# Experts' second layer of a mixture-of-experts stage: full-precision products replaced by split fp32r products, with the results of GELU split in two

## What is computed

```python
h   = gelu(einsum('ecd,edf->ecf', xb, fc_w) + fc_b)      # 192 -> 768
out = einsum('ecf,efd->ecd', h, pj_w) + pj_b             # 768 -> 192, the second layer
y   = einsum('nec,ecd->nd', cb_weight, out)              # weighted back to the tokens
```

## Time and profile before

| what | value |
|---|---|
| runs (3): median, lowest, highest | 1009.45, 1009.11, 1009.66 us |
| the profiled execution's own time | 1016.04 us |
| its span, first to last instruction | 1014.3 us |
| mean granted TensorE clock, share of full speed | 0.923 |

### The profile page before, as it was taken

How to read it: one execution, slowest core, us unless ns; L and a number is a source line. 1 busy time by engine, 2 the same in 40 slices (tenths; PEclk the granted TensorE clock), 3 DMA queues, 4 the chain that set the end, 5 groups by cost and what they waited for, 6 DMA issues and landing times.

```text
span 1014.3 us, 21583 instructions
## 1 busy us (share of the span) xinstructions
PE 897.5 (88%) x7037; PEld 698.7 (69%) x7038; DVE 653.3 (64%) x3059; ACT 647.0 (64%) x1379; POOL 504.4 (50%) x549
## 2 busy tenths in 40 slices
PE   3387979999999979999999999367999999999996
PEld 2255556566666656677776776256999999999896
DVE  1676888998998877778877776673344343343341
ACT  2047778886989888988888889165345345344441
POOL 7677746765221201144234333415677677667654
PEclk8577998998999979999999999758999999999999
DMA  7234332322110200010011102427455456554443
GB/s 201 60 75 79 48 63 42 60 62 29 33 32 8 58 1 2 2 38 17 23 39 38 38 3 73 74 56 110 59 109 109 65 110 90 87 109 92 55 50 32
DMA packets 63300, 59.12 MB, mean 58 GB/s; under 512 B 17471, under 2 KB 54242, under 8 KB 63202
## 3 DMA queue, kind: packets, MB, share of 16 engines
q0 software_dynamic: 26624, 29.20, 20.0%
q1 hardware_dynamic: 36386, 28.44, 10.9%
q10 hardware_dynamic: 192, 0.26, 0.1%
HBM read 35.18 MB, written 16.39 MB: 51 GB/s over the span
## 4 chain that ended last, share of the span: by engine, by line
PE 62%; DVE 13%; ACT 5%; issue 3%; POOL 1%; DMA 0%; another core or an unknown queue 0%; POOLq 0%; DVEq 0%; ACTq 0%
PE ps_scores L798 14%; PE ps_ring L790 11%; PE ps_ring L1068 10%; PE ps_ring L798 6%; PE ps_ctx L927 5%; PE ps_scores L910 5%; PE ps_scores L1068 4%; PE ps_scores L913 4%; DVE probs L1456 2%; DVE probs L1470 1%; ACT probs L1170 1%; DVE k L1377 1%; PE ps_ring L873 1%; PE ps_ctx L790 1%; DVE probs L1450 1%
## 5 line engine op out<-in xcount | busy, mean ns | idle before, releaser
L1292 ACT ACTIVATE probs<-ps_scores,fc_bias 128x512 f32<-128x512 f32 (+1 forms) x144 | 88.7, 617 | 172.2 <-PE ps_scores L798 153.9
L661 POOL DMA_INDIRECT out<-z_t,slots_now x80 | 127.8, 1597 | 83.7 <-DVE z_t L1809 59.6
L1152 ACT ACTIVATE prob_t<-ps_ring 128x512 f32<-128x512 f32 x192 | 114.5, 597 | 36.0 <-PE ps_ring L790 35.4
L790 PE MATMUL ps_ring<-ident,probs 128*128 128x128 f32 x768 | 127.6, 292 | 9.0 <-DVE x_hi L1348 4.5
L1177 ACT ACTIVATE probs<-probs,neg_max 128x128 f32<-128x128 f32 x384 | 120.9, 398 | 2.6 <-DVE neg_max L1456 2.5
L1161 ACT ACTIVATE square<-ps_scores 128x512 f32<-128x512 f32 x192 | 104.9, 601 | 25.4 <-PE ps_scores L910 20.0
L1068 PE MATMUL ps_ring<-work,probs 128*128 128x192 f32 x672 | 114.5, 326 | 0.0
L790 PEld LDWEIGHTS ps_ring<-ident,probs 128*128 128x128 f32 x768 | 90.8, 147 | 34.1 <-issue 15.5
L1456 DVE CUSTOM_DVE_ANT_0 probs<-ps_scores,causal 128x128 f32<-128x128 f32 x384 | 88.5, 286 | 39.6 <-PE ps_scores L913 39.1
L1068 PEld LDWEIGHTS ps_ring<-work,probs 128*128 128x128 f32 x672 | 109.3, 190 | 0.1
L798 PE MATMUL ps_scores<-x_hi,fc_hi 128*128 128x512 f32 (+1 forms) x288 | 105.1, 371 | 3.8 <-DVE x_hi L1793 2.6
(11 more groups left out here) (232 smaller groups left out, 2074.0 us busy)
## 6 DMA issues: line engine op xcount, KB each, us to landing
work<-pj_w SPq DMA_DIRECT2D x8, 576.0 KB
k<-k_signed SPq DMA_DIRECT2D x136, 32.0 KB
token_in<-xin SPq DMA_DIRECT2D x8, 384.0 KB, 3.3
out<-resid SPq DMA_DIRECT2D x8, 384.0 KB, 4.2
vals<-fc_w SPq DMA_DIRECT2D x8, 384.0 KB
vals<-fc_w SPq DMA_DIRECT2D x16, 192.0 KB
k<-k_signed POOLq DMA_DIRECT2D x40, 32.0 KB, 2.0
out<-z_t,slots_now POOLq DMA_INDIRECT x80, 3.6
```

Of the source, the lines that this page charges most:

```text
L661: gp.indirect_dma_start(out[:, :], bass.IndirectOffsetOnAxis(slots_now[:, u, 1, t:t + 1], 0), slot_y[:, o, :], None, compute_op=ALU.add).t ...
L790: return pe.transpose(dst, src, ident[0:n, 0:n])
L1152: sc.activation(prob_t[:, s % 2, :, :], src.rearrange("p (h q) -> p h q", h=4), ACT.Exp if p is mag else ACT.Copy).then_inc(ring_free[i], 1)
L1292: sc.activation(hidden[:, c % 2, f_, 0:128 * nt], ps_scores[:, i, 0:128 * nt], ACT.Gelu, bias=fc_bias[:, e, f_:f_ + 1]).then_inc(gelu_done ...
```

## The change

The second layer is written as a split product too. The second weights are rounded by ACT to fp32r (`second_weights_high`) and DVE writes the rest beside them (`second_weights_low`), so that `pj_split` holds for each of six blocks 192 rounded columns and 192 columns of rest. Each of GELU's results is rounded by ACT (`hidden_high`, an ACT copy of the block to `hid_hi`), one block behind the GELUs, and DVE subtracts (`hidden_low`, to `hid_lo`). For each tile PE then multiplies the six rounded blocks by all 384 columns and the six rests by the first 192 columns: 12 matmuls, in the order five rounded, six rests, the last rounded. The rest's rest is left out. `add_bias` adds both halves of the 384 columns of the result, with one more DVE instruction. SP waits for `pj_low` in place of `pj_used`. The tiles' places in memory are rearranged so that `hid_hi`, `hid_lo` and `pj_split` lie where the attention's q, k and the tiles `xin`, `w_hi`, `square` were.

```diff
@@ SyncE
-                sp.wait_ge(pj_used[e % 2], e // 2 + 1)
+                if e > 1:
+                    sp.wait_ge(pj_low, e - 1)
                 load_second_layer(e)
@@ TensorE
             def second_layer(r, u, e, c):
                 t0, nt = CHUNKS[c]
                 if c == 0:
-                    pe.wait_ge(pj_loaded[u], 16 * r + 16)
+                    pe.wait_ge(pj_low, e + 1)
+                order = ([(hid_hi, hid_high, f_) for f_ in range(FF_CHUNKS - 1)]
+                         + [(hid_lo, hid_low, f_) for f_ in range(FF_CHUNKS)] + [(hid_hi, hid_high, FF_CHUNKS - 1)])
...
-                    for f_ in range(FF_CHUNKS):
+                    for k, (part, made, f_) in enumerate(order):
                         if t == t0:
-                            pe.wait_ge(gelu_done[f_ % FC_RING], e * 6 + 2 * c + f_ // FC_RING + 2)
-                        last = pe.matmul(ps_y[i][:, 0:HID], hidden[:, c % 2, f_, tok], pj_w_sb[:, u, f_, :],
-                                         start=(f_ == 0), stop=(f_ == FF_CHUNKS - 1))
+                            pe.wait_ge(made, e * 18 + 6 * c + f_ + 1)
+                        n = 2 * HID if part is hid_hi else HID
+                        last = pe.matmul(ps_y[i][:, 0:n], part[:, f_, tok], pj_split[:, u, f_, 0:n],
+                                         start=(k == 0), stop=(k == 2 * FF_CHUNKS - 1))
@@ ScalarE, in gelus
                     sc.activation(hidden[:, c % 2, f_, 0:128 * nt], ps_scores[:, i, 0:128 * nt], ACT.Gelu,
                                   bias=fc_bias[:, e, f_:f_ + 1]).then_inc(gelu_done[i], 1)
+                    if f_ > 0:
+                        hidden_high(e, c, f_ - 1)
+                hidden_high(e, c, FF_CHUNKS - 1)
+
+            def hidden_high(e, c, f_):
+                tok = slice(0, 128 * CHUNKS[c][1])
+                act.wait_ge(gelu_done[f_ % FC_RING], e * 6 + 2 * c + f_ // FC_RING + 2)
+                apart(act)
+                sc.activation(hid_hi[:, f_, tok], hidden[:, c % 2, f_, tok], ACT.Copy).then_inc(hid_high, 1)
+
+            def second_weights_high(n, u):
+                act.wait_ge(pj_loaded[u], 16 * n + 16)
+                sc.activation(pj_split[:, u, :, 0:HID], pj_w_sb[:, u, :, :], ACT.Copy).then_inc(pj_high, 1)
@@ ScalarE, in expert
                     expert_weights_high(e + 1, 1 - u)
+                    second_weights_high(r + u, 1 - u)
@@ VectorE, in add_bias
-                        ve.tensor_tensor(slot_y[:, o, :], ps_y[i][:, 0:HID], pj_bias[:, e, :], ALU.add
+                        ve.tensor_tensor(slot_y[:, o, :], ps_y[i][:, HID:2 * HID], pj_bias[:, e, :], ALU.add
+                                         ).then_inc(y_begun, 1)
+                        dve.wait_ge(y_begun, CAP_TILES * e + t + 1)
+                        ve.tensor_tensor(slot_y[:, o, :], slot_y[:, o, :], ps_y[i][:, 0:HID], ALU.add
                                          ).then_inc(y_free[i], 1)
@@ VectorE
+                def hidden_low(e, c):
+                    tok = slice(0, 128 * CHUNKS[c][1])
+                    for f_ in range(FF_CHUNKS):
+                        dve.wait_ge(hid_high, e * 18 + 6 * c + f_ + 1)
+                        apart(dve)
+                        ve.tensor_tensor(hid_lo[:, f_, tok], hidden[:, c % 2, f_, tok], f(hid_hi[:, f_, tok]),
+                                         ALU.subtract).then_inc(hid_low, 1)
+
+                def second_weights_low(e, u):
+                    dve.wait_ge(pj_high, e + 1)
+                    apart(dve)
+                    ve.tensor_tensor(pj_split[:, u, :, HID:2 * HID], pj_w_sb[:, u, :, :],
+                                     f(pj_split[:, u, :, 0:HID]), ALU.subtract).then_inc(pj_low, 1)
+
                 def expert(e, u, more):
+                    hidden_low(e, 0)
                     split_x(e, u, 1)
                     add_bias(e, u, 0)
                     if more:
                         split_weights(e + 1, 1 - u)
+                        second_weights_low(e + 1, 1 - u)
+                    hidden_low(e, 1)
                     split_x(e, u, 2)
                     add_bias(e, u, 1)
+                    hidden_low(e, 2)
                     if more:
                         split_x(e + 1, 1 - u, 0)
                     add_bias(e, u, 2)
```

More of the change, by code:

```diff
@@ L192, in tower_kernel @@
         resid = sb("resid", [128, SEQS, HID])
-        xin = sb("xin", [128, SEQS, WITH_GATE])
+        with ExitStack() as attention_only:
+            early = lambda name, shape, dt=F32: attention_only.enter_context(nc.sbuf_tensor(name, shape, dt))
+            q_of = [early(f"q{u}", [128, BLOCKS, GROUP, 128]) for u in range(2)]
+            k_of = [early(f"k{u}", [128, BLOCKS, 2, GROUP, 128]) for u in range(2)]
+            xin = early("xin", [128, SEQS, WITH_GATE])
+            w_hi = early("w_hi", [128, 2, 2, 384], F32R)
+            square = early("square", [128, 2, 4, 2, 128])
+        low_hot_at = sb("low_hot", [128, BLOCKS * GROUP * 128], F32R)
+        high_hot_at = sb("high_hot", [128, BLOCKS * GROUP * 128], F32R)
+        fc_hi = sb("fc_hi", [128, 2, 2, FF], F32R)
+        fc_lo = sb("fc_lo", [128, 2, 2, FF], F32R)
+        hid_hi = sb("hid_hi", [128, FF_CHUNKS, 512], F32R)
+        hid_lo = sb("hid_lo", [128, FF_CHUNKS, 512], F32R)
+        pj_split = sb("pj_split", [128, 2, FF_CHUNKS, 2 * HID], F32R)
         logits = sb("logits", [128, 2, EXPERTS])
@@ L239, in tower_kernel @@
                      for u in range(2)]
-        with ExitStack() as attention_only:
-            early = lambda name, shape: attention_only.enter_context(nc.sbuf_tensor(name, shape, F32))
-            q_of = [early(f"q{u}", [128, BLOCKS, GROUP, 128]) for u in range(2)]
-            k_of = [early(f"k{u}", [128, BLOCKS, 2, GROUP, 128]) for u in range(2)]
-        low_hot_at = sb("low_hot", [128, BLOCKS * GROUP * 128], F32R)
-        high_hot_at = sb("high_hot", [128, BLOCKS * GROUP * 128], F32R)
-        fc_hi = sb("fc_hi", [128, 2, 2, FF], F32R)
-        fc_lo = sb("fc_lo", [128, 2, 2, FF], F32R)
         vals_of = [vals[:, :, :, :], work[:, 2560:4096].rearrange("p (s h d) -> p s h d", s=GROUP, h=HEADS)]
@@ L412, in tower_kernel @@
         pj_loaded = [sem(f"pj_loaded{u}") for u in range(2)]
-        pj_used = [sem(f"pj_used{u}") for u in range(2)]
+        pj_high = sem("pj_high")
+        pj_low = sem("pj_low")
+        hid_high = sem("hid_high")
+        hid_low = sem("hid_low")
+        y_begun = sem("y_begun")
         x_loaded = [sem(f"x_loaded{c}") for c in range(3)]
@@ L790, in transpose, with split_product @@
                 return pe.transpose(dst, src, ident[0:n, 0:n])
-            def split_product(dst, x, w_cols, v, begun=None):
+            def split_product(dst, x, w_cols, v):
                 pairs = ((x[0], w_cols[0]), (x[0], w_cols[1]), (x[1], w_cols[0]), (x[2], w_cols[2]),
@@ L798, in split_product @@
                     last = pe.matmul(dst, lhs, rhs, start=(k == 0), stop=(k == 4))
-                    if begun is not None and k == 0:
-                        last.then_inc(begun, 1)
                 return last
@@ L1016, in _ @@
                 pe.sem_inc(y_free[i], 1)
-            pe.sem_inc(pj_used[0], 1)
             for i in range(FC_RING):
@@ L1051, in first_layer @@
                                   (fc_hi[:, u, 0, col], fc_lo[:, u, 0, col], fc_hi[:, u, 1, col],
-                                   fc_lo[:, u, 1, col]), False,
-                                  begun=pj_used[1 - u] if c == 0 and f_ == 0 else None).then_inc(fc_full[i], 1)
+                                   fc_lo[:, u, 1, col]), False).then_inc(fc_full[i], 1)
             def second_layer(r, u, e, c):
@@ L1293, in gelus, with expert @@
                                   bias=fc_bias[:, e, f_:f_ + 1]).then_inc(gelu_done[i], 1)
-            def expert(e, u, more):
+                    if f_ > 0:
[9 more added lines that the diff above has]
+                sc.activation(pj_split[:, u, :, 0:HID], pj_w_sb[:, u, :, :], ACT.Copy).then_inc(pj_high, 1)
+            def expert(r, u, more):
+                e = r * 2 + u
                 if u == 0:
@@ L1310, in _ @@
             whole_x(0, 0)
+            second_weights_high(0, 0)
             with act.Fori(0, EXPERTS // 2 - 1, 1) as r:
-                expert(r * 2, 0, True)
-                expert(r * 2 + 1, 1, True)
-            expert(EXPERTS - 2, 0, True)
-            expert(EXPERTS - 1, 1, False)
+                expert(r, 0, True)
+                expert(r, 1, True)
+            expert(EXPERTS // 2 - 1, 0, True)
+            expert(EXPERTS // 2 - 1, 1, False)
         @blk.vector
@@ L1823, in experts @@
                 split_x(0, 0, 0)
+                second_weights_low(0, 0)
                 expert(0, 0, True)
```

2 lines of the change are left out of this document (removed).

## The result

The changed kernel takes 1027.29 us (median of 4 runs, 1024.20 to 1030.69) against 1009.56 of the kernel before on the same chip (4 runs, 1009.11 to 1011.33): ratio 1.0159, 95% interval 1.0129 to 1.0189. The two medians by themselves lie 17.7 us apart (1.0176, inside that interval). The forecast was 1034, range 1012 to 1047, slower with a chance of 0.84. The profiled execution took 1024.62 us, its span is 1022.9. Executed once more among the experiments, the change had a ratio of 1.0176 (1.0146 to 1.0205).

A forecast was written before the change was run, and what follows sets the result against it. PE alone was taken to set the pace. Chunks' 1.6 + 0.75 + 0.60 = 2.95 us per expert, 23.6 for 8, 24.4 with end effects, gave 1040.4 profiled, 1034 as median; bounds 1018 to 1046, range 1012 to 1047.

The forecast's parts named there:

- PE's gain: Second layer: a tile takes 1.73 us instead of 1.92, ten tiles and 8 experts make 15 us if PE never waits.
- chunk 1: An expert's second block, four tiles: 16.41 us instead of 15.66, 0.75 more, from waits for the sixth rest and a bank.
- the sixth rest: DVE's last subtraction of a chunk, needed by its first tile: PE waits 0.93 us in chunk 1, 1.37 in chunk 2.
- a PSUM bank: Chunk 1's fourth tile waits 0.56 us for a bank that DVE's additions free only after splitting x.
- chunk 2: An expert's third block: 15.85 us instead of 15.25, 0.60 more, with a wait of 1.37 and no second wait.
- all is covered: Rival: copies and rests land before PE asks, the tile's gain stays, -15 us, 994; chance 0.13.
- gain and waits cancel: Rival: the whole time stays within 2 us of 1009; chance 0.03.
- 384 columns cost as 512: Rival, second layer: a tile takes 2.08 us, 4.6 more per expert, 37.6 in all, 1047; chance 0.07.
- Products without overhead: Rival, second layer: matmuls stream at 2.4 GHz, a tile takes 1.44 us, 14.8 more in all, 1024; chance 0.07.
- chunk 0: An expert's first block, two tiles: 1.6 us longer, since DVE finishes x of chunk 1 later.
- a chain of hand-overs: GELU, ACT copy, DVE subtraction, PE: each hand-over 0.15 us, 0.2 for a matmul inside PE's block.
- The base: Whole kernel: the median of runs lies 6.6 us below the profiled execution's 1016.04, so 1040.4 becomes 1033.9.

The follow-up runs named there:

- e1: The changed kernel without ACT's copies and DVE's subtractions of the hidden values, only to measure: 37.20 us per expert, ratio to before 0.985.
- e2: The changed kernel without DVE's subtractions, copies kept, rests' products reading `hid_hi`, only to measure: 39.31 us per expert, ratio to before 1.0034.
- e10: The changed kernel with PE, DVE and POOL lists reordered (gathers ahead of output additions) and chunk 0's second layer in plain fp32: ratio to before 0.9959.
- e9: The changed kernel with PE and DVE orders moved and POOL's gathers ahead of output additions, all chunks split: 38.89 us per expert, ratio to before 0.9998.
- e4: The changed kernel with only PE's second-layer order changed, a chunk's first two tiles side by side: 40.47 us per expert, ratio to before 1.0117.
- e6: The changed kernel with PE and DVE orders moved and chunk 0's second layer in plain fp32, gathers unmoved: 39.67 us per expert, ratio to before 1.0025.
- e8: The changed kernel, orders untouched, with only chunk 0's second layer back in plain fp32: 40.37 us per expert, ratio to before 1.0107.

## Why the prediction was right, and where it was off

**Direction and mechanism: right.** PE's gain was forecast at 1.9 per expert; e1 shows 1.99, partly by luck, as said there. It is lost to waits of the named kinds: x of chunk 1 (L1816), the sixth rest at the first tile of chunks 1 and 2 (L1844), a PSUM bank (L1831), with the clock at 1.00. One wait was not forecast by name, for the last copies at chunk 2's first tile (L1308, 8 times); it lies inside the wait for the sixth rest.

**Rivals.** That all is covered falls by the result itself, and by e1 and e2, which give back 4.1 us when copies and rests are left out; that gain and waits cancel falls by the interval, which excludes 1. That 384 columns cost as 512 falls by e1 and by their starts, 0.174 apart where 512 columns have 0.233. Products without overhead: groups of PE of the change, 700 to 1000 us, give only durations (347 ns, 276 ns), but in starts a tile is 1.72, as 6 x 0.178 + 6 x 0.11 makes it, not 1.44.

**The size: 16 to 18 us, not 24.** Measured per expert 41.33 - 39.19 = 2.14, forecast 2.95. Eight experts make 17.1, and the stages' difference is 15.7 (first profiles) or 18.4 (second). Of the 0.81 between forecast and measurement the wait for the sixth rest makes 0.31, the bank 0.10, chunk 0 0.16 and the first layers 0.17; the rest is rounding and 0.01 per tile. By chunks:

| | forecast | measured | what was mis-sized |
|---|---|---|---|
| chunk 0 | +1.6 | +1.42 | subtractions end 5.94 after the expert's start, not 6.14; the weights take 0.76, not 0.90; x takes 2.87, not 2.68 |
| chunk 1 | +0.75 | +0.42 | wait for the sixth rest 0.79, not 0.93; bank 0.46, not 0.56; first layer 7.07, not 7.12 |
| chunk 2 | +0.60 | +0.28 | wait 1.20, not 1.37; first layer 7.00, not 7.12 |

The step that failed is the price of a chain of hand-overs, and DVE's rows of the change show both halves of it, first in chunk 0, then at the end of chunk 1's subtractions:

```profile
771.84 0.76 DVE L1844 TENSOR_TENSOR hid_lo<-probs,hid_hi 128x256 fp32r<-128x256 f32 x2 [0.24 <-ACT hid_hi L1308]
772.52 0.16 DVE L1797 TENSOR_TENSOR row_w<-low_hot 128x4 f32<-128x4 f32 x1
...
773.36 0.55 DVE L1813 CAST x_hi<-k_signed 128x512 fp32r<-128x512 f32 x1
...
775.81 0.42 DVE L1816 TENSOR_TENSOR x_hi<-x_full,x_hi 64x256 fp32r<-64x256 f32 x1
```
```profile
785.08 1.29 DVE L1844 TENSOR_TENSOR hid_lo<-probs,hid_hi 128x512 fp32r<-128x512 f32 x2 [0.47 <-ACT hid_hi L1308]
```

The waits came where they were put; their size was off. Two subtractions of 512 take 1.29, so that the second starts 0.60 after the first, though one alone takes 0.691; of 256, 0.76 and 0.34. I had put them end to end (0.684, 0.425). And the last one ends at 786.37 while PE's sixth rest starts at 786.42: a hand-over of 0.05 where I took 0.2. Measured from the end of the first layer, 783.43, the chain was forecast to give the rest at +3.25 and gave it at +2.99. The bound for this was in the text (subtractions overlapping by 0.07, hand-overs of almost nothing; low end 1018); the kernel lies between that end and the value taken. The durations of single instructions were right, as the groups of the change by shape show (700 to 1000 us), beside the earlier trace rows:

```profile
L1308 ACT ACTIVATE hid_hi<-probs 128x512 fp32r<-128x512 f32 x88 | 53.1, 621 | 0.0
L1308 ACT ACTIVATE hid_hi<-probs 128x256 fp32r<-128x256 f32 x42 | 16.8, 420 | 0.0
...
L1844 DVE TENSOR_TENSOR hid_lo<-probs,hid_hi 128x512 fp32r<-128x512 f32 x89 | 59.8, 691 | 41.0 <-ACT hid_hi L1308 40.6
L1844 DVE TENSOR_TENSOR hid_lo<-probs,hid_hi 128x256 fp32r<-128x256 f32 x42 | 17.3, 425 | 13.7 <-ACT hid_hi L1308 13.7
```

The Trainium skill (VectorE: DVE Perf Modes, the section on the TRN2 errata) has two formulas for the time of such an operation on N elements: (N + 151)/0.96 ns for an fp32 `tensor_tensor`, 691 and 424 ns, which the durations match, and 58 + N cycles of a 0.96 GHz clock, which it calls too small for one operation. The second gives 594 and 327 ns. The page doesn't say that this is the distance of two starts, but in these rows it comes near the 0.60 and 0.34 between the starts of two in a row; an estimate with both formulas for the pair, 1.285 and 0.751, would have been within 0.01.

**The first layer** seems shorter where its first matmul follows an fp32r product and not an fp32 one: in the earlier trace rows that matmul is recorded as 0.53 long, in the change as 0.40 (the row at 792.44). e10 has both cases in one kernel, chunk 1 behind fp32 and chunk 2 behind fp32r:

```profile
774.97 0.53 PE L807 MATMUL ps_scores<-x_hi,fc_hi 128*128 128x512 f32 x1
775.34 0.39 PE L807 MATMUL ps_scores<-x_hi,fc_lo 128*128 128x512 f32 x1
...
789.89 0.41 PE L807 MATMUL ps_scores<-x_hi,fc_hi 128*128 128x512 f32 x1
790.15 0.39 PE L807 MATMUL ps_scores<-x_hi,fc_lo 128*128 128x512 f32 x1
```

The second matmul starts 0.37 after the first behind fp32 and 0.26 behind fp32r. But behind fp32 the first one also starts 0.03 after the last fp32 record, where these records are otherwise 0.163 apart: the end of the fp32 product is booked on the first layer. So a tile in fp32 costs 12 x 0.163 = 1.95 and not 1.92, and a tile gains 0.23 and not 0.19. The sum had both numbers from a cut at this place, and left out some 0.1 per chunk.

**The base.** I subtracted 6.6 us to come from the profiled execution to the median. In the second profile of before (1010.43, 5.6 less than the first) the first expert is 1.6 shorter and the start of the experts 3.9 earlier: nearly all of that difference lies outside the steady experts, so that to subtract it was right. The end was sized well too: the last chunk and what follows it take 24.4 us in the change and 22.9 and 22.7 in the profiles of before, 1.5 to 1.7 more, where the sum had 0.60 + 0.44 + 0.39.

## What to carry to other kernels

A split into rounded part and rest shortens PE's work only where both parts are at hand: against 2.0 us gained per expert 4.1 were lost, though over 20 us neither ACT (12.9) nor DVE (16.0) was full. Ask of each engine's list what is issued after the last block's result, and move everything else ahead of the first or behind the hand-over: three moves in lists that leave the products as they are took 41.3 us to 38.8. Where a block is too short to hide the hand-over (chunk 0), leave it unsplit (e10's 38.0 against e9's 38.9), and when PE becomes faster look at once at who was only just in time before, here the gathers.

## What was not expected

**The experts' start follows attention's clock.** Ahead of the experts all these kernels do the same work but for two instructions on the first second weights, yet the experts' first matmul starts between 683.2 and 694.8 us. It goes, roughly, with the clock granted to PE between 150 and 250 us (the two profiles with 0.90 below still differ by 4.5 us), here for the change, before (second profile), before (first) and e4, in this order, where the experts start at 683.2, 686.5, 690.3 and 694.8:

```profile
150.00:250.00 100.00, 94.30 (x847) 62.45 (x848) 93.80 (x459) 84.39 (x150) 67.65 (x67) 0.98 0.30 52
```
```profile
150.00:250.00 100.00, 94.39 (x828) 61.56 (x823) 89.96 (x441) 81.04 (x144) 65.72 (x62) 0.93 0.28 49
```
```profile
150.00:250.00 100.00, 94.53 (x811) 61.51 (x811) 88.13 (x433) 79.24 (x142) 65.87 (x63) 0.90 0.29 51
```
```profile
150.00:250.00 100.00, 91.26 (x780) 59.15 (x779) 86.64 (x419) 77.12 (x138) 66.16 (x63) 0.90 0.30 52
```

It fits with this that single times of one kernel scatter by 5 us either way while before's experts, from the second on, are 39.19 each; that the clock is the cause was not tried. A granted clock between the two levels of 1.2 and 2.4 GHz is a mixture of them over the stretch; no other level stands in the clock records of these traces. e10's stage is 7.1 us shorter than before's second, its whole span 4.2 (1004.5 against 1008.7), because its experts begin 2.9 later at a clock of 0.92; the medians of 12 and 23 executions differ by 4.2 too. It isn't this one profile alone: the clock over the whole span is 0.922 in the middle of e10's 12 executions (0.915 to 0.927) and 0.926 in the middle of the 23 of before beside them (0.922 to 0.932). Another 0.4 us lies outside the span, which in the median is 2.1 us shorter than the device time in e6, e8 and e10, the kernels with chunk 0 in fp32, and 1.7 or 1.8 in the others. What in the variant would do either stays open.

**Small matmuls have a price of their own.** The prediction took 0.11 for 192 columns from attention's rows, and it holds here. In the timeline of the changed kernel above, six rests of 192 columns take 0.65 in starts (787.69 to 788.34), 0.108 each, and five products of 384 columns 0.87 (786.82 to 787.69), 0.174 each. By columns, from 0.233 for 512 (30 in the 7.00 of chunk 2's first layer), 384 make 0.175 and 192 only 0.087. Whether the loading of weights sets the pace of the narrow ones was not tried.
